# Query and key parts in one tile with joint transfers, weight jobs requested at other places, zero points converted once, in a fused attention and gated-network kernel

## The reference

```
xn = layernorm(x)
qkv = clip(xn @ Wqkv.T, -8, 8);  q, k, v = split(qkv)
q = layer_norm(q) * q_w + q_b;   k = layer_norm(k) * k_w + k_b
scores = q @ k.T * 16**-0.5 + slope[head] * (pos_k - pos_q), causal
s = softmax(scores) @ v @ Wout.T
w = (int_weight - zero) * scale                  # gate, up and down
g = silu((silu(xn @ gate) * (xn @ up)) @ down)
out = x + s * g
```

## Time and profile before

| what | us |
|---|---|
| median of 3 runs | 1349.84 |
| lowest and highest run | 1346.81, 1351.06 |
| the profiled execution's own time | 1358.14 |
| its span, first to last instruction | 1356.1 |
| TensorE busy | 1213.4 (89%) |
| VectorE, ScalarE, POOL busy | 741.4, 617.3, 501.5 |
| DMA packets of q1 | 85744, 110.14 MB, 31.6% of 16 engines |

### The profile page before, as it was taken

One profiled execution on the slowest core, in us unless ns is written; L12 is line 12 of the kernel. 1 busy time (PEld: TensorE's weight loads), 2 busy tenths in 40 slices (PEclk: granted clock), 3 DMA queues, 4 the chain that ended last, 5 costly groups with the idle time before them and its releaser, 6 DMA issues. The chain is left out here.

```text
span 1356.1 us, 22935 instructions
## 1 busy us (share of the span) xinstructions
PE 1213.4 (89%) x7168; PEld 801.3 (59%) x7168; DVE 741.4 (55%) x1153; ACT 617.3 (46%) x923; POOL 501.5 (37%) x512
## 2 busy tenths in 40 slices
PE   6899986889888888888888876999999999999997
PEld 5677743434433434444434324888888878888886
DVE  6778895656666666566666514235433542453223
ACT  3333313556565555556566563433343343333332
POOL 2756630212121121112121122455455545545553
PEclk9999976889899889888899877999999999999999
DMA  6343554654566354756655332010210021002000
GB/s 214 95 141 94 158 147 111 152 119 121 152 104 144 94 115 108 159 110 136 125 112 137 96 109 84 11 54 0 89 37 33 1 94 52 12 18 75 0 1 31
DMA packets 112248, 123.63 MB, mean 91 GB/s; under 512 B 29648, under 2 KB 83408, under 8 KB 112080
## 3 DMA queue, kind: packets, MB, share of 16 engines
q1 hardware_dynamic: 85744, 110.14, 31.6%
q10 hardware_dynamic: 26464, 12.98, 3.5%
HBM read 92.80 MB, written 29.88 MB: 90 GB/s over the span
## 5 line engine op out<-in xcount | busy, mean ns | idle before, releaser
L266 DVE TENSOR_REDUCE mx<-bank 128x1 f32<-128x512 f32 (+3 forms) x608 | 371.1, 658 | 213.1 <-PE bank L278 212.1
L922 ACT ACTIVATE pr<-pair 128x1024 f32<-128x1024 f32 (+3 forms) x384 | 297.0, 810 | 267.0 <-PE pair L1012 237.2
L1136 POOL TENSOR_TENSOR ws_lo<-w_f,ws_hi 128x512 fp32r<-128x512 f32 x168 | 247.0, 1497 | 262.2 <-ACT ws_hi L1177 262.2
L1296 DVE TENSOR_TENSOR sg<-pair,sg 128x512 f32<-128x512 f32 x56 | 38.7, 692 | 260.0 <-ACT sg L1224 260.0
L1359 PE MATMUL pair<-xc_hi,ws_lo 128*128 128x512 f32 x448 | 175.2, 391 | 1.4 <-DVE xc_lo L1279 1.4
L1359 PE MATMUL pair<-xc_lo,ws_hi 128*128 128x512 f32 x448 | 175.0, 391 | 0.0
L1359 PE MATMUL pair<-xc_hi,ws_hi 128*128 128x512 f32 x448 | 174.8, 390 | 0.0
L1224 ACT ACTIVATE sg<-pair 128x512 f32<-128x512 f32 x56 | 33.5, 598 | 235.7 <-PE pair L1359 235.7
L276 PE MATMUL bank<-identb,behind 128*128 128x512 bf16 x128 | 60.4, 472 | 69.9 <-DMA ks<-in_krows 39.2
L895 POOL TENSOR_TENSOR w_f<-w_f,zst 128x896 f32 (+1 forms) x24 | 50.1, 2087 | 195.1 <-ACT zst L937 195.1
L278 PE MATMUL bank<-xin_c,s_sb 108*128 108x128 bf16 (+3 forms) x576 | 115.7, 307 | 5.4 <-DVE mx L266 4.9
(11 more groups left out here) (95 smaller groups left out, 1936.3 us busy)
## 6 DMA issues: line engine op xcount, KB each, us to landing
stk<-parts ACTq DMA_DIRECT2D x16, 768.0 KB, 5.7
zst<-in_z_all SPq DMA_DIRECT2D x24, 448.0 KB, 4.3
sst<-in_s_all SPq DMA_DIRECT2D x24, 448.0 KB, 5.1
w_f<-in_w_all SPq DMA_DIRECT2D x24, 448.0 KB, 7.1
oscr<-ot SPq DMA_DIRECT2D x32, 256.0 KB, 2.5
xin_c<-in_x SPq DMA_DIRECT2D x32, 256.0 KB, 2.7
s_sb<-stk SPq DMA_DIRECT2D x96, 64.0 KB
xin_c<-stk SPq DMA_DIRECT2D x96, 64.0 KB
```

The lines of the kernel that those rows point to most:

```text
L266: dve.tensor_reduce(dst, b[:, 0:n_heads * w].rearrange("p (j c) -> p j c", c=w), AX.X, ALU.max).then_inc(m_free, 1)
L922: act.activation(pr[e % NPR][:, 2 * p:2 * p + 2, 0:w], pair[p][:, :, 0:w], ACT.Exp, scale=SCALE)\
L1136: return pool.tensor_tensor(dst, src, hi.bitcast(F32), ALU.subtract)
L1296: dve.tensor_tensor(sg[s][:, :], pair[s][:, 1, :], sg[s][:, :], ALU.mult).then_inc(h_mul, 1)
```

## The change

1. `s_sb` and `xin_c` become one tile `xs`, and `qs1` and `ks1` become `qk1`. A slot `qk_s[s]` holds, for each half, four heads of queries and then four of keys. All reads change to that layout.
2. The parts of the keys are stored in reversed order (high in place 2, low in place 0). High times low, middle times middle and low times high then have the same place on both sides, so one transfer brings a block of 16 rows for queries and keys; the other three blocks still take two. `load` has 10 transfers in place of 14.
3. `stk` has another order of dimensions, and ScalarE stores a pair of tiles with four transfers of 64 rows in place of two of 128.
4. The constant rows of queries and keys are copied once, from memory to memory, into `crow`, 16 rows for both sides together, by four transfers that SP requests in tile 1 of block 1. SP waits for them before the first load.
5. The zero points of all jobs are loaded once (24 rows), converted once by ScalarE at the end of block 1 and stored to `zscr`, from where the jobs fetch them. `convert` no longer converts zero points.
6. In odd groups SP requests the second weight job behind the load of half 0, not ahead of it.
7. ScalarE converts at steps 1 and 10 in even groups and at step 5 in odd ones. POOL does the first job of an even group between the two chains.

The core of the diff:

```diff
@@ load
-            p0 = (i % 2) * 64
-            for r, both in enumerate(((0, 0), (1, 0), (2, 0), (0, 1), (1, 1), (0, 2))):
-                rows = slice(r * HD, (r + 1) * HD)
-                src = stk[:, bass.ds(i // GROUPS, 1), bass.ds(p0, 64), bass.ds((i % GROUPS) // 2, 1), :, :]
-                for a, dst in enumerate((qs[s][rows, b, :, :], ks[s][rows, :, cols])):
-                    part = src[a].rearrange("a (j c) k w s -> w c (a j) (k s)", j=GH)[both[a]]
-                    sp.dma_start(dst, part[:, :, cols]).then_inc(stk_in[s][b], 16)
...
+            src = stk[bass.ds(i // GROUPS, 1), s, :, :, :, bass.ds((i % GROUPS) // 2, 1), :, cols]
+            part = src.rearrange("b a j c k w s -> w (b c) (a j) (k s)")
+            for w in range(3):
+                rows = slice(w * HD, (w + 1) * HD)
+                sp.dma_start(qk_s[s][rows, b, :, :], part[w]).then_inc(stk_in[s][b], 16)
+            for r, (wq, wk) in enumerate(((0, 2), (1, 2), (0, 1))):
+                rows = slice((3 + r) * HD, (4 + r) * HD)
+                sp.dma_start(qk_s[s][rows, b, 0:GH, :], part[wq][:, 0:GH, :]).then_inc(stk_in[s][b], 16)
+                sp.dma_start(qk_s[s][rows, b, GH:2 * GH, :], part[wk][:, GH:2 * GH, :]).then_inc(stk_in[s][b], 16)
+            sp.dma_start(qk_s[s][96:112, b, :, :], crow[bass.ds(i % GROUPS, 1), :, :, cols].rearrange("a p j s -> (a p) j s"))\
               .then_inc(stk_in[s][b], 16)
@@ block 1, SP, tile 1
+                            sp.dma_start(z_int[:, :], z_all).then_inc(zall_in, 16)
+                            sp.dma_start(crow[:, 0:12, 0:GH, :], qrows).then_inc(crow_in, 16)
+                            sp.dma_start(crow[:, 12:16, 0:GH, :], krows[:, 0:4, :, :]).then_inc(crow_in, 16)
+                            sp.dma_start(crow[:, 0:15, GH:2 * GH, :], krows).then_inc(crow_in, 16)
+                            sp.dma_start(crow[:, 15:16, GH:2 * GH, :], krows[:, 14:15, :, :]).then_inc(crow_in, 16)
@@ block 1, ScalarE
                     for a in range(2):
-                        dst = stk[a, bass.ds(c // 4, 1), :, :, :, bass.ds((c % 4) * 2 * P, 2 * P)]
...
+                        for g in range(2):
+                            dst = stk[bass.ds(c // 4, 1), g, a, :, :, :, :, bass.ds((c % 4) * 2 * P, 2 * P)]
...
+                act.wait_ge(zall_in, 16)
+                act.activation(z_flt[:, :], z_int[:, :], ACT.Copy).then_inc(zall_conv, 1)
@@ block 2, SP
-                    if not last:
-                        half_job(3 * ip + (1, 3)[s])
+                    if s == 0:
+                        half_job(3 * ip + 1)
                     if last is None:
 
                         sp.wait_ge(s_full[1], full(i, LOW_KEYS - 1))
                         apart(sp, "sp")
                         load(sp, i + 2, s, 0)
+                    if s == 1 and not last:
+                        half_job(3 * ip + 3)
@@ block 2, POOL
                     chain(pool, dneg1, 2 * i + 1)
+                    if s == 0:
+                        job(3 * ip)
                     if not last:
...
-                    job(3 * ip + (0, 2)[s])
-                    if s == 0:
-                        job(3 * ip + 1)
+                    job(3 * ip + 1 + s)
@@ block 2, ScalarE
-                    act.activation(w, w.bitcast(I32), ACT.Copy)
-                    act.activation(zst[:, :], zst[:, :].bitcast(I32), ACT.Copy).then_inc(z_conv, 1)
+                    act.activation(w, w.bitcast(I32), ACT.Copy).then_inc(z_conv, 1)
...
-                        if e == JOB_AT:
-                            convert(3 * ip + (0, 2)[s])
+                        if e in JOBS_AT[s]:
+                            convert(3 * ip + (2 if s else JOBS_AT[s].index(e)))
...
-                    if s == 0:
-                        convert(3 * ip + 1)
```

62 lines of the change are left out of this document (33 added, 29 removed).

## The result

The changed kernel takes 1327.55 us, median of 4 runs (1326.33 to 1333.2), beside 1350.12 for the kernel before (4 runs, 1346.81 to 1351.06): a ratio of 0.9866, 95% interval 0.9817 to 0.9914. It is faster by 22.6 us where 83.8 were forecast, and lies outside the range. The profiled executions took 1326.48 and 1358.14 us; between their spans lie 31.6 us. I use the spans to place the time, and the medians for what is gained.

The account below looks back on a forecast made before the run. Group-start waits for half 0 of queries and keys, with the low clock behind them, cost some 100 us. Sum: -60.6 - 37.6 - 5.1 - 7 + 10 + 10.5 + 6 = -83.8, from 1349.84 to 1266 us; range 1248 to 1276.

Parts of the forecast that it names:

- Stores of parts: Stage one, ScalarE: two more 0.71 us requests every two tiles hide behind its 2.55 us wait for TensorE; 0, uncovered 11.
- Copies: Stage one, SP queue: 2.1 MB of constant-row copies make tile 4's input 9 us late, two thirds of it paid: +6 us.
- slow copies: Rival, stage one: constant-row copies run at half the rate, making the tile 23 us late; 1279 us in all, chance 0.14.
- Load gaps: Attention group starts: TensorE's waits for half 0 of the next queries and keys go, except the first: -60.6 us.
- Low clock: Attention stage: the lower granted clock behind the 14 later group-start gaps goes with those gaps: -37.6 us.
- Offset rows: Even groups: POOL finishes the job by the next group's start, so TensorE's waits for these rows go: -5.1 us.
- Last group: End of attention: POOL's chain comes about 4 us earlier, a 3.0 us wait goes, SP's last job is requested earlier: -7 us.
- Zeros: 24 conversions leave an idling ScalarE; the one conversion and store hide behind SP's barrier wait at stage one's end: 0.
- First weight job: Group 0, step 1: ScalarE's conversion waits for a job requested behind the first load, and TensorE behind it: +10 us.
- Later weight jobs: Conversions at step 1 of even and step 5 of odd groups wait for late jobs, 0.5 and 1 us each: +10.5 us.
- jobs late: Rival, attention stage: jobs land later, ScalarE stands some 3 us per group more, TensorE behind it: +35, 1300 us, chance 0.16.
- The stall-free group: Attention stage: a group without the load gap, low clock and offset-row waits takes 30.8 us, against 38.05 between starts.

Follow-up runs that it names:

- e9: The kernel before with each of its two stores of parts cut into rows 0 to 63 and 64 to 127, nothing else: 1360.12 us, ratio 1.0172.
- e6: The changed kernel with conversions at step 3 for step 1 in even groups and step 6 for step 5 in odd ones: 1306.32 us, ratio 0.9716.
- e7: e6 with the two query stores ahead of the next tile's splitting on ScalarE and the two key stores behind it: 1282.18 us, ratio 0.9518.
- e12: e8 with the first read of half 1 two places later and the constant-row copies requested near the end of stage one: 1277.8 us, ratio 0.9539.
- e4: The changed kernel with the four copies of the constant rows requested near the end of stage one, not at its start: 1325.61 us, ratio 0.9845.
- e8: e2 with conversions at steps 3 and 6 in place of 1 and 5: 1278.18 us, ratio 0.9508.
- e13: The kernel before with each store of parts cut into even and odd rows, 64 each over all 128 partitions: 1347.02 us, ratio 1.0033.
- e2: The changed kernel with 128-row stores, each cut in two along columns, and plain blocks loaded apart (13 requests a load): 1324.54 us, ratio 0.9833.

## Why the prediction was wrong, point by point

**Stores of parts, 0 (11 with the cover gone).** This is the step that failed worst: 17 us in e9, where nothing but the halves was changed, 24 from e6 to e7, and most of the 22.3 here. The prediction priced two more requests at 0.71 us, the first one in the earlier trace rows, and asked whether ScalarE's 2.55 us would cover 1.4. The transfers had changed from 128 rows to one half of the partitions, whose price no row of before could show: four of them hold ScalarE 5.4 us, with 1.7 and 2.1 for the third and fourth. And it looked only at the engine that requests. What TensorE paid for is the tile of x beside them, which lands 3 us later, with the clock behind the gap. The "bound" of 11 was the cost of the same wrong 0.71 without cover; a bound for a transfer of a new shape must allow it to be slower per byte, and to slow what runs beside it.

**Copies, +6.** Too high, as far as the runs tell. The wait near 35 us came, 3.94 us long and ending at 38.33, but no pair of runs shows more than 3.1 us of it at the end of the stage, and e7 and e12 show nothing. The *slow copies* rival did not happen. The tile behind them was 2.9 us later than in e4, and 3 to 5 in the other traces, not 23, and the data moved at 165 to 271 GB/s in the windows from 26 to 38 us. The rule on the number of DMA engines, named there from the Trainium skill ("DMA: Bandwidth & Descriptors", section "Why a DMA increments its semaphore by 16 and not by 1"), did not have the effect that I derived from it.

**Load gaps, -60.6.** Nearly right: 52 us of waits went (65.9 to 13.7), and none at half 0 is left but the first, 7.6, of which I expected 2.5 less. What stayed is 6 us in six even groups at the first read of **half 1**, where the prediction saw "slack 2 us, no cost" and which it named as a sign of being wrong. The read comes when it said, 9.2 us behind the group's start, but half 1 landed at +10.5 (531.64 behind 521.13), not at +7: its last request leaves at +3.5 and lands 7 us later.

**Low clock, -37.6.** Right in kind, too large. Over 270 to 750 the granted clock was 0.92 before; the sum of the shares missing in 2 us windows over that stretch is 39.5 us there and 10.2 in the changed kernel. By TensorE's busy time with the same 3616 matmuls over the 14 periods, 457.3 us before, 434.3 after and 421.5 in e8, 23.0 us came back. The rest lies in six stretches of some 3 us that reach 1.2 GHz. Two of them are behind two short waits in a row in even groups, as behind the rows at 531.64 and 533.14 above:

```profile
533.00:535.00 2.00, 1.86 (x6) 0.61 (x6) 0.69 (x1) 1.09 (x2) 0.00 (x0) 0.69 0.00 0
535.00:537.00 2.00, 2.00 (x18) 0.63 (x18) 0.69 (x1) 1.06 (x2) 0.00 (x0) 0.50 0.00 0
```

The other four are behind waits for exponentials, of 3.12 us (301.29), 1.52 (327.09), 1.60 (436.39) and 1.67 (638.05). But the clock stayed up behind four like pairs (at 399, 467, 601 and 669 us) and behind single waits of 1.50 to 1.89 us (370, 504, 572 and 706). The prediction took it from the 1.69 us at 494.57 that small waits leave the clock up. That is true of some waits of this size and not of others, and the length of the wait alone does not say which; what does stays open.

**Offset rows, -5.1.** Wrong: 11.2 us for 8.1, and 7.3 for 5.1 without the last group. POOL was in time as forecast, and ScalarE requests the rows 5.0 us behind the group's start in even groups and in odd ones (526.11 behind 521.13). It is the transfer that is slow: the 12 KB land 6.6 to 7.1 us later in even groups, which makes TensorE wait 0.9 to 1.4 us, and 5.0 to 5.2 in odd ones, which makes it wait 0.25 to 0.41. The prediction had no term for the landing. **Last group, -7:** -5.9. POOL's chain begins 1.1 us behind the group's start for 6.9, and SP requests its last job at +1.2 for +7.0, both as forecast; the wait of 3.0 us for the rows did not go, it is 3.8.

**Zeros, 0.** Nothing shows a cost: e7 has them and ends stage one at 210.9, before at 211.2, and SP's barrier wait, 8.4 us, still covers their store.

**First weight job, +10.** Nearly right: group 0 is 9.8 us longer, with the first gap 0.2 us shorter and not 2.5. ScalarE stood 9.37 us, TensorE 7.87 behind it.

```profile
255.77 0.95 ACT L953 ACTIVATE w_f<-w_f  x1 [9.37 <-DMA w_f<-in_w_all]
```

**Later weight jobs, +10.5.** ScalarE's waits for them are 19.9 - 9.4 = 10.5 us, the number forecast; their price was not. e6 takes nearly all of them away and the 14 periods shrink by 18 us. The wait of ScalarE was a good estimate of itself and a poor one of what the kernel pays: TensorE waits 14.6 us for exponentials in these periods, and four of the six low stretches of the clock lie behind such waits. Of the rivals this is *jobs late*, at half its price.

**The stall-free group, 30.8,** was right (30.85 in e8). The misses add up. In stage one it is 22.3 for 6, that is 16.3. In group 0, which holds the first gap, it is 9.8 for 10 - 2.5, that is 2.3. In the 14 periods it is 33.83 for 31.5 (37.97 less a fourteenth of 58.1 + 37.6 + 5.1 - 10.5), that is 32.3, of which 14.6 are clock, 7.3 offset rows, 6.0 half 1 and 4.1 exponentials (14.6 for 10.5). In the last group it is 1.1. That is 52.0 of the 52.2 between the forecast change (-83.8) and that of the spans (-31.6). Another 9 lie between the spans' difference and the medians': the profiled execution of before was 8 us over its median, that of after 1 us under. The forecast took a difference made against one execution off the median of others, though it had noticed the 8.3 us.

## What to carry to other kernels

When a transfer changes shape, price its new shape and not the count of requests: rows of one half of the partitions are a different transfer from as many rows spread over all of them. And ask what else is landing at that time: the engine that requests was held longer here, but TensorE paid for a neighbour's tile. Before naming the wait that costs, go back from the idle engine to the wait that ended last. Before moving a request behind others, write down which engine stands at its landing and what is queued behind that engine; where only the order changed here, the old wait came back under another name and the kernel got slower. Place a consumer that blocks an in-order engine by the landing measured with everything ahead of it, plus a step.

## What the runs showed of the hardware

Stores of 384 KB from 64 rows took a median of 6.4 us to land from one half of the partitions and 4.4 from every second row (e9, e13); four of them in a row held the engine that requests them 5.3 and 3.7 us. Two alone took 1.26 (e7); of four in a row the third and fourth are held, 1.7 and 2.1 us in the changed kernel. A tile of 256 KB that another queue requests while such a set is under way landed 7.1 us after its request beside halves (7.7 in e9), 4.1 beside two stores of 128 rows, 3.9 beside every second row (e13) and 2.8 beside two halves (e7). Behind waits of 1.5 to 1.9 us the granted clock fell to 0.50 for some 3 us in three places of the changed kernel and stayed up in four. From 270 to 760 us the changed kernel's DMA engines were busy 0.73 of the time at 138 GB/s, e2's with the plain blocks loaded apart 0.55 at the same 138 GB/s: the transfers of 128 pieces into 16 rows keep the engines busier for their bytes. What that costs beside the later offset rows of e6, which e8 does not have, wasn't measured by itself.
